# Weighed values and their sums moved by DMA inside SBUF, and the context divided there

## What is computed

```python
xn = layernorm(x)                        # rows of 512
q, k, v = xn @ Wq, xn @ Wk, xn @ Wv      # 32 query heads; 8 key/value heads in layers 0, 2, 3
p = softmax(q @ k.T / 4)                 # causal in layers 0, 2, 3; rotary q, k there
ctx = p @ v                              # [256, 16] of each head, side by side: [256, 512]
x = x + (ctx @ Wo) * ffn(xn)             # ffn differs by layer
```

## Time and profile before

| | |
|---|---|
| Median of 3 runs | 1331.58 us (1330.56 to 1336.55) |
| The profiled execution | 1332.45 us, of which its span is 1330.7 us |
| TensorE, busy share of the span | 91% |
| VectorE, ScalarE, GpSimd | 61%, 49%, 29% |
| Mean granted clock of TensorE | 0.98 of full speed |
| Small matmuls of the values, line 869 | 2048 in 128 groups |
| Transposes, lines 880 and 888 | 256 and 128, each 128x128 |

### The profile page before, as it was taken

The page is one execution under the profiler, slowest core; times in us unless marked ns, Lnnn a source line. Parts: engine busy times, 40 slices in busy tenths (PEclk is TensorE's granted clock), DMA queues, the critical chain, the costliest instruction groups (busy, mean ns, idle before and its releaser), DMA issues.

```text
span 1330.7 us, 22702 instructions
## 1 busy us (share of the span) xinstructions
PE 1216.5 (91%) x8860; PEld 900.0 (68%) x8860; DVE 808.3 (61%) x1322; ACT 652.6 (49%) x1106; POOL 385.9 (29%) x460
## 2 busy tenths in 40 slices
PE   4999999999999999979999999999899889898897
PEld 3788876666656556546777787776666666676664
DVE  8743467665675645674655566536776776765444
ACT  3333357555454555554333333336665655565653
POOL 1000125333210101021344434405532342424443
PEclk9999989999999999979999999899999999999999
DMA  6000000110000100001242222120001001000001
GB/s 254 0 1 0 1 34 3 48 58 2 1 2 2 36 1 1 26 25 48 72 142 95 95 72 80 64 80 3 2 2 40 2 2 34 1 25 23 2 1 63
DMA packets 15259, 48.07 MB, mean 36 GB/s; under 512 B 2858, under 2 KB 6959, under 8 KB 14388
## 3 DMA queue, kind: packets, MB, share of 16 engines
q1 hardware_dynamic: 15156, 46.63, 10.1%
HBM read 44.00 MB, written 2.10 MB: 35 GB/s over the span
## 4 chain that ended last, share of the span: by engine, by line
PE 71%; DVE 14%; ACT 8%; issue 4%; DMA 2%; POOL 0%; POOLq 0%; DVEq 0%; ACTq 0%; SPq 0%
PE bank L650 18%; PE bank L766 14%; PE bank L680 8%; PE bank L909 8%; PE bank L869 6%; PE bank L817 4%; PE bank L783 3%; DVE negmax L1816 3%; ACT probs L1381 3%; PE bank L849 2%; ACT pv L1389 2%; PE bank L880 2%; DMA W_lo_whole<-in_w 2%; PE bank L797 1%; PE bank L826 1%
## 5 line engine op out<-in xcount | busy, mean ns | idle before, releaser
L1816 DVE TENSOR_REDUCE negmax<-bank 128x4 f32<-128x1024 f32 (+1 forms) x256 | 250.3, 1017 | 77.0 <-PE bank L826 66.2
L1381 ACT ACTIVATE probs<-bank 128x1024 f32<-128x1024 f32 (+1 forms) x256 | 218.0, 865 | 46.0 <-PE bank L849 37.7
L2023 POOL TENSOR_SCALAR_AFFINE_SELECT probs<-probs 128x512 f32<-128x512 f32 x192 | 125.9, 666 | 292.3 <-ACT probs L1381 292.1
L1966 POOL TENSOR_TENSOR W_lo<-W_lo_whole,W_hi 128x1536 fp32r<-128x1536 f32 x28 | 98.4, 3516 | 155.8 <-ACT W_hi L1132 155.8
L817 PE MATMUL bank<-kT,qT 64*128 64x256 f32 (+1 forms) x1024 | 110.5, 312 | 30.1 <-DVE negmaxT L1834 8.8
L817 PEld LDWEIGHTS bank<-kT,qT 64*128 64x128 f32 x1024 | 81.4, 191 | 65.9 <-issue 33.2
L869 PE MATMUL bank<-probs,V 128*32 128x256 f32 (+1 forms) x2048 | 119.6, 352 | 6.6 <-DVE negmax L1816 5.1
L1389 ACT ACTIVATE pv<-bank 128x256 f32<-128x256 f32 x128 | 49.2, 384 | 154.1 <-PE bank L869 153.6
L849 PE MATMUL bank<-qT,kT 64*128 64x256 f32 (+1 forms) x640 | 113.4, 384 | 3.7 <-DVE h_lo_whole L1638 1.6
L1132 ACT ACTIVATE W_hi<-W_lo_whole 128x1536 fp32r<-128x1536 f32 x28 | 41.7, 1488 | 130.6 <-DVE W_lo_whole L1592 130.6
L650 PE MATMUL bank<-xT_hi,W_hi 128*128 128x512 f32 x224 | 91.7, 410 | 5.6 <-ACT silu L1145 4.5
(11 more groups left out here) (205 smaller groups left out, 2692.3 us busy)
## 6 DMA issues: line engine op xcount, KB each, us to landing
W_lo_whole<-in_w SPq DMA_DIRECT2D x28, 768.0 KB, 4.1
Wqkv_lo_whole<-in_Wqkv SPq DMA_DIRECT2D x6, 768.0 KB, 6.7
Wo_lo_whole<-in_Wo SPq DMA_DIRECT2D x4, 1024.0 KB, 4.9
Wqkv<-in_Wqkv SPq DMA_DIRECT2D x2, 1536.0 KB, 7.5
Wdown_whole<-in_Wd SPq DMA_DIRECT2D x1, 2816.0 KB, 14.6
x<-in_x SPq DMA_DIRECT2D x4, 512.0 KB, 5.4
out<-x SPq DMA_DIRECT2D x8, 256.0 KB, 2.0
V_lo_whole<-in_V SPq DMA_DIRECT2D x1, 1408.0 KB, 5.8
```

The costliest lines, as they stand in the source:

```text
L1381: nc.scalar.activation(A[l].probs[gi % 2][kb][:, :, q0 - kb * A[l].probs1:].rearrange("p (b h) q -> p b h q", b=2), B.tensor(key)[:, :, 0: ...
L1816: v.tensor_reduce(A[l].negmax[u % 2][:, qb, :].rearrange("p (b h) -> p b h", b=2)[:, :, 2 * g:2 * g + 2], B.tensor(key)[:, :, 0:2 * nk].re ...
L1966: gp.tensor_tensor(lo, whole, hi.bitcast(F32), ALU.subtract).then_inc(w_low.sem, 1)
L2023: gp.affine_select(out=blk, in_=blk, compare_op=ALU.is_ge, fill=0.0, base=0, pattern=[[0, 4], [1, P]], channel_multiplier=-1).then_inc(cau ...
```

## The change

No transposes of the context are left: `turn_context`, `turn_rows`, `take_rows`, `ctxr`, `ctxT`, `recip` and the VectorE version of `context_low` go. The weighed values keep their layout, heads by queries, which is the layout in which `project_out` wants them; only the padding between the heads has to be closed, and the sum has to reach every one of the 16 partitions of its head.

- SyncE moves them: for each group, once `pv` is written, `move_values` issues five DMAs inside SBUF. Four take the 16 partitions of one head each to `parts`, the fifth copies each head's sum 16 times into `sums` (a source step of 0). Two groups fill the 128 partitions of `parts` and `sums`: a **pair**. SyncE's own program becomes a `slot(r, G)` too, with `place_maxima` and the weight loads set between the moves.
- VectorE handles a pair at a time, in the even slots from G = 4 on: a reciprocal of `sums` (128x256, in place) and a product `parts` x `sums` (128x256, all in SBUF) into a ring of 6 pairs, `ctx_whole`.
- In the GQA layers ScalarE copies the pair to `ctx_hi` (128x256, behind `take_pv` in the same slot) and GpSimd subtracts for `ctx_lo` (128x256, last in its slot). `project_out` waits for the low parts of the sequence's four pairs.
- `weigh_values` uses bank 6 in place of 4 and 7, up to U = 13 (bank 4 after that). `take_pv` waits for the moves of two groups ago before it overwrites `pv`.
- The residual's product goes into `gate` in place; the split of layer 3's Wo moves from four slots of unit 10 to three; at the ends of the runs the last two pairs are handled in `ffn2` and `ffn3` (`project_out` of layer 3's last sequence one chunk later).

```diff
-def values_bank(l, U, g):
-    return 7 if not GQA[l] and g % 2 == 0 and U + 1 + g // 2 < RUN else 4
+def values_bank(U, g):
+    return 6 if U + 2 + g % 2 < RUN else 4
...
+def pair_scaled(G):
+    return (G - 4) // 2 if G >= 4 and G % 2 == 0 else None
...
@@ TensorE
-            def turn_context(r, G, slot, bank=None):
...
-            def turn_rows(l, b, tau, bank):
...
-                pe.wait_ge(*B.emptied(("ctxT", l, b, tau)))
+                pe.wait_ge(*(ctx_low if GQA[l] else ctx_scaled).at(l, 4 * (b + 1)))
...
@@ ScalarE
+                if G >= 2:
+                    act.wait_ge(*moved(r, G - 2))
                 nc.scalar.activation(A[l].pv[gi % 2][:], B.tensor(key)[:, 0:SEQ], copy).then_inc(B.empties(key), 1)
...
+            def context_high(r, q):
+                l, qi = pair(r, q)
+                if GQA[l]:
+                    act.wait_ge(*ctx_scaled.at(l, qi + 1))
+                    nc.scalar.activation(ctx_hi[r][:, q % RING, :], ctx_whole[r][:, q % RING, :], copy).then_inc(ctx_high.sem, 1)
...
                 if G >= 1:
                     take_pv(r, G - 1)
+                if pair_scaled(G) is not None:
+                    context_high(r, pair_scaled(G))
...
@@ VectorE
+            def context(r, q):
+                l, qi = pair(r, q)
+                dve.wait_ge(*moved(r, 2 * q))
+                dve.wait_ge(*moved(r, 2 * q + 1))
+                sums = A[l].sums[q % 2][:]
+                v.reciprocal(sums, sums).then_inc(rs_ready.sem, 1)
+                if q >= RING:
+                    ll, qq = pair(r, q - RING)
+                    dve.wait_ge(*B.filled(("O", ll, qq // 4, 1)))
+                dve.wait_ge(*rs_ready.at(l, qi + 1))
+                v.tensor_tensor(ctx_whole[r][:, q % RING, :], A[l].parts[q % 2][:], sums, ALU.mult).then_inc(ctx_scaled.sem, 1)
...
-                if G >= 2:
-                    context(r, G - 2)
+                if pair_scaled(G) is not None:
+                    context(r, pair_scaled(G))
...
@@ GpSimd
+            def context_low(r, q):
+                l, qi = pair(r, q)
+                if GQA[l]:
+                    pool.wait_ge(*ctx_high.at(l, qi + 1))
+                    gp.tensor_tensor(ctx_lo[r][:, q % RING, :], ctx_whole[r][:, q % RING, :],
+                                     ctx_hi[r][:, q % RING, :].bitcast(F32), ALU.subtract).then_inc(ctx_low.sem, 1)
...
@@ SyncE
+            def move_values(r, G):
+                l, gi = group(r, G)
+                q = G // 2
+                sp.wait_ge(*B.emptied(("PV", l, gi)))
+                if q >= 2:
+                    ll, qq = pair(r, q - 2)
+                    sp.wait_ge(*ctx_scaled.at(ll, qq + 1))
+                pv, row, first = A[l].pv[gi % 2], SEQ, 64 * (G % 2)
+                for i in range(4):
+                    load(A[l].parts[q % 2][first + HD * i:first + HD * (i + 1), :], pv[32 * i:32 * i + HD, :], pv_moved[G % 2])
+                load(A[l].sums[q % 2][first:first + 64, :], bass.AP(pv, HD * row, [[32 * row, 4], [0, HD], [1, SEQ]]), pv_moved[G % 2])
...
+            def slot(r, G):
+                U, g = divmod(G, GROUPS)
+                if g == 2 and U + 1 < RUN:
+                    place_maxima(r, U + 1)
+                if r == 0 and g == 3:
+                    loads_0(U + 1)
...
+                if G >= 1:
+                    move_values(r, G - 1)
+                if r == 1 and g == 3:
+                    loads_1(U + 1)
```

More of the change, by code:

```diff
@@ L503, in program @@
         m_rows = [sem(f"max_rows_placed{i}") for i in range(2)]
+        pv_moved = [sem(f"weighed_values_moved{i}") for i in range(2)]
         out_done = sem("output_stored")
@@ L857, in weigh_values @@
                 key = ("PV", l, gi)
-                ps = claim(key, values_bank(l, *divmod(slot, GROUPS)))
+                ps = claim(key, values_bank(*divmod(slot, GROUPS)))
                 if CAUSAL[l]:
@@ L872, in weigh_values @@
                 ins.then_inc(B.fills(key), 1)
-            def turn_context(r, G, slot, bank=None):
[L875 to L881, removed]
-            def turn_rows(l, b, tau, bank):
-                key = ("ctxT", l, b, tau)
-                ps = claim(key, bank)
-                pe.wait_ge(*B.emptied(("ctx", l, 8 * b + 7)))
-                for c in range(KC):
-                    ins = nc.tensor.transpose(ps[:, c * P:(c + 1) * P], A[l].ctxr[b % 2][:, tau, c * P:(c + 1) * P], ident[:])
-                ins.then_inc(B.fills(key), 1)
             def project_out(l, b, tau, bank):
@@ L1012, in ffn2 @@
                 weigh_values(0, last, last)
-                turn_context(0, last - 1, last)
-                turn_context(0, last, last, 2)
                 down(2, 0)
-                turn_rows(1, SEQS - 1, 0, 3)
-                turn_rows(1, SEQS - 1, 1, 2)
                 down(2, 1)
@@ L1068, in ffn3 @@
                     if e == CHUNKS3_EARLY:
-                        turn_context(1, last - 1, last)
                         weigh_values(1, last, last)
-                    if e == CHUNKS3_EARLY + 1:
-                        turn_context(1, last, last)
-                        for tau in range(2):
-                            turn_rows(3, SEQS - 1, tau, 6 + tau)
-                    if e == CHUNKS3_EARLY + 2:
+                    if e == CHUNKS3_EARLY + 3:
                         for tau in range(2):
@@ L1259, in ffn2 @@
                 gate_silu(2, CHUNKS2_EARLY)
-                for tau in range(2):
-                    take_rows(1, SEQS - 1, tau)
                 weights_high(CHUNKS2_EARLY + 1)
@@ L1306, in ffn3 @@
                     if e == CHUNKS3_EARLY + 1:
-                        for tau in range(2):
-                            take_rows(3, SEQS - 1, tau)
+                        context_high(1, RUN * GROUPS // 2 - 2)
+                    if e == CHUNKS3_EARLY + 2:
+                        context_high(1, RUN * GROUPS // 2 - 1)
                         bias2_high()
@@ L2037, in slot @@
                     wqkv_low_part(3, g)
-                if r == 1 and U == 10:
-                    wo_low_part(3, g)
+                if r == 1:
+                    for c in WO3_SLOTS.get((U, g), ()):
+                        wo_low_part(3, c)
                 if r == 1 and (U, g) in SPLIT3_SLOTS:
@@ L2133, in place_maxima, with loads_0 @@
                          m_rows[u % 2])
-            for hh in range(2):
-                load(Wqkv_whole[0][hh][:], a["Wqkv0"][:, :, hh, :], qkv_in[0][hh])
-            sp.wait_ge(*B.filled(("out", 0, TILES - 1)))
-            load(Wo_whole[0][:], a["Wo0"], wo_in)
-            for U in range(RUN):
-                place_maxima(0, U)
+            def move_values(r, G):
[9 more added lines that the diff above has]
+                load(A[l].sums[q % 2][first:first + 64, :], bass.AP(pv, HD * row, [[32 * row, 4], [0, HD], [1, SEQ]]), pv_moved[G % 2])
+            def loads_0(U):
                 if U in (4, 5):
```

176 lines of the change are left out of this document (81 added, 95 removed).

## The result

The changed kernel takes 1365.7 us (median of 4 runs, 1359.2 to 1368.2) against 1332.7: ratio 1.0237, 95% interval 1.0193 to 1.0281. The forecast was 1307, with a range up to 1344: it is slower by 33 us, and out of the range.

What follows compares the result with a forecast made beforehand. TensorE, busy 91% of the span, was taken to bound the kernel. 1332.45 - 57 (transposes, bank) + 27.5 (ScalarE's hold) + 5 (ends) = 1308, so about 1307 us against the runs' median; range 1272 to 1344.

Steps and rivals of the forecast that it cites:

- The sizes of the new instructions: Per pair on VectorE: reciprocal 1.8 us, product 0.42; ScalarE's high copy 0.38; SyncE's issue 0.63 us.
- VectorE's growth: VectorE's busy time goes from 808 to about 870 us, net, still under TensorE.
- ScalarE's hold: In plain slots the high copy waits for VectorE's product, delaying exponentials and projection: 1.1 us for 25 pairs, 27.5 us.
- TensorE's shed work: The context transposes leave TensorE: 28.2 us for 128 pairs and 14.0 us for 128 more, 42.2 us saved.
- The bank: Values in bank 6: row scores no longer wait for the copy (10 us), values not for maxima (5 us).
- rival E: The bank's part doesn't come, the wait for `pv` moves to the second `scores_cols`: 15 us lost, 1322 us; 8%.
- SyncE, at nothing: SyncE's five moves a group, 3.2 us, 403 us in all, stay hidden if an issue stays under about 0.8 us.
- `ffn2`'s boundary: The last pair reaches the projection 2.3 us late, cancelled by transposes and a wait that go, about 2 us.
- The clock: Granted TensorE clock, 1.00 in the windows read; the forecast would be wrong if it fell.
- C: Products reading two SBUF tiles collide with GpSimd, adding 1.3 us to each plain pair's 1.1: 1343 us; 16%.
- B: VectorE isn't in the way: reciprocal 0.43 us, pair 0.85 us, only the ends lost: 1280 us; 24%.
- D: SyncE paces the slots if an issue takes from 1.1 us on: plus 67 us, about 1399 us; 6%.

Runs made afterwards that it cites:

- b_recip: The kernel before plus a VectorE reciprocal of 256 elements a partition in each even slot from the fifth on, its result unread; 1392.1 us.
- e_recip8: The changed kernel with the reciprocal taken over 8 of the 256 columns only; 1294.2 us.
- e_high_late: The changed kernel with ScalarE's high copies moved behind the odd slot's exponentials, and the low parts with them; 1360.6 us.
- the better order: The changed kernel with high copies behind the odd slot's exponentials and maxima taken ahead of the pair in even units; 1333.4 us; with transposes put back 1350.8.
- the four kernels of length and order: Reciprocal over 256 or 8 columns: 1366 and 1294 us in the order of the change, 1333 and 1297 in the better order.
- the same fold of 4: The changed kernel, sums folded to 32 partitions of 64 elements, inverted, spread by four DMAs: 1528.7 us; with a slot between each DMA and its reader 1333.8.

## Why the prediction was wrong

- **The sizes of the new instructions: right.** Reciprocal 1.74 us for 1.8, product 0.426 for 0.42 as a median (0.555 as a mean), high copy 0.42 for 0.38, an issue 0.59 to 0.60 for 0.63, VectorE's waits for the moves 8 us for 5. The Trainium skill ("VectorE: DVE Perf Modes", "First, the fixed hardware budget") has a reciprocal iterated 8 times, from which the estimate was 2.1 us. The runs give 542, 943 and 1744 ns for 64, 128 and 256 elements: 6.3 ns for each further element, by that estimate's clock some six cycles rather than eight. (The recorded 5.3 ns of the earlier trace rows should read 5.4; the time taken, 1.8, doesn't rest on it.)
- **VectorE's growth at no price, "still under TensorE": the step that failed.** The growth itself, 63 us forecast, was 76; 8 of the 13 more are the product's longer mean. By the rate of `b_recip`, 0.56, it is worth 43 us; I gave it nothing apart from ScalarE's hold. The share of busy time (61%) was read as room, though the argument on the stalls shows that VectorE's order, not its sum, is what TensorE meets: in each slot key copies, maxima and other evictions stand behind whatever is added. `e_recip8` and `b_recip` show it from both sides: 71 us gone with the reciprocal's length, 59 us added by a reciprocal alone. I named ScalarE's queue behind the pair and did not name VectorE's own: `take_max`, in every even slot with g = 2, with `scores_rows` waiting for it, 8.8 to 30.3 us.
- **ScalarE's hold, 27.5 us: the place right, the size by luck, the worth wrong.** The projection's wait for the exponentials rose by 27.1 us, but not as 25 stalls of 1.1 us: in the timelines 15 of its 29 stalls, 25 us of the 32, stand behind a high copy that was held, and with the reciprocal nearly gone, where I had it at nothing, 24.4 us stay (`e_recip8`). Taking it away alone gave 5 us (`e_high_late`); it is worth its price only together with the maxima.
- **TensorE's shed work, 42.2 us: the count right, the worth a third.** Put back as fillers of 28 and 25 us of busy time, it costs 13 us, 17 in the better order. The price from the chain was read where TensorE runs without a gap; in a kernel that now has 177 us of gaps part of it, I take it, only widened them.
- **The bank, 15 us: nothing.** The first link came true (7.4 to 1.3 us of wait), and the wait moved on to L793 and the projection. That is what rival E said, with another place.
- **SyncE, at nothing: 6 us** (3 to 10), by a way that stays open. **`ffn2`'s boundary**, 2.3 us late and cancelled: TensorE stood 6.6 us there once; 2.8 of them are VectorE's `h_lo`, just ahead of the pair, which ran 3.50 us for 0.69 beside a GpSimd subtraction of 3.42.
- **The clock.** I wrote that a falling clock would make me wrong, and gave it no price. It fell from 0.980 to 0.954. Between `e_recip8` and the changed kernel the same matmuls differ by 30 us of busy time; by the two mean clocks (0.974 and 0.954) some 24 of them would be the clock's, an estimate.

A ledger in the order of the change, from single edits: -13 (transposes), +43 (VectorE's 76 us at 0.56), +6 (moves), 0 (bank) gives 1333 + 36 = 1369; measured 1366. That it fits is in part luck: its rates come from edits at both ends, it has no term of its own for ScalarE's hold, and the four kernels of length and order show that its terms don't add. Of the rivals, C had the right sign and a third of the loss (1343), by another mechanism: collisions stayed rare (14 of 64 products, 8 us), and the hold was not its price. B's reciprocal of 0.43 us is not what ran; `e_recip8`, with a shorter one still, took 1294 for B's 1280. D fell with the issues, 0.59 us where it needed 1.1.

## What to carry to other kernels

An engine at 60% of the span is not free if each of its queued items has a reader on the critical engine: price what is added by the items queued behind it in the same slot, one by one, on its own queue as well as on the next engine's. Where two waits come from one late instruction, remove both before judging either; alone each removal looked worthless. A DMA inside SBUF between two steps of an in-order engine is cheap if a slot of other work lies between issue and reader, and ruinous if not (1529 for 1334 us at the same fold of 4).

## What the runs showed of the hardware

- A VectorE reciprocal takes some 0.14 us plus 6.3 ns an element of the free size, whatever the number of partitions: 542 ns for 32x64, 943 for 16x128, 1744 for 128x256, 1749 for 64x256. Folding rows over partitions shortens it.
- GpSimd's power takes 41.1 us for 128x256.
- A gap of TensorE of 1.65 us was followed by 4.4 us of matmuls at the 1.2 GHz level, another of 2.06 us was not. Over a kernel, 105 us of extra work on VectorE showed up half as TensorE's idle time (+29) and half as more busy time for the same matmuls (+28), at a mean clock of 0.958 for 0.980.
